# Two-way attention and experts on one core: the output projection of a batch and its residual issued one round later, ahead of the next projections

## The reference

```python
qkv   = layernorm(x) @ Wqkv + bqkv
qkv_a = ctx @ Wqkv_aux + bqkv_aux
q, k, v = split_heads(qkv);  _, ka, va = split_heads(qkv_a)      # 16 heads of 8
p  = softmax(q @ k.T * scale);  pa = softmax(q @ ka.T * scale)
gate = sigmoid(g)                                               # one per head
att = (p @ v) * (1 - gate) + (pa @ va) * gate
x = x + tanh(g_xattn) * (att @ Wo + bo)
# then: x = x + tanh(g_ffn) * experts(layernorm(x)), 64 experts, 8 per token, and one shared expert
```

## Time and profile before

| what | value |
|---|---|
| time, median of 3 runs | 875.36 us (871.0 to 877.55) |
| time of the profiled execution | 874.03 us |
| its span in the trace | 872.2 us |
| granted TensorE clock | 1.0 of full speed throughout |
| PE / DVE / ACT / POOL busy | 832.4 / 690.8 / 565.8 / 637.7 us |
| batch 2, round 0 to batch 31, round 3 | 56.1 to 301.0 us of the span |

### The profile page before, as it was taken

The page is one execution under the profiler, slowest core; times in us unless marked ns, Lnnn a source line. Parts: engine busy times, 40 slices in busy tenths (PEclk is TensorE's granted clock), DMA queues, the critical chain, the costliest instruction groups (busy, mean ns, idle before and its releaser), DMA issues.

```text
span 872.2 us, 20170 instructions
## 1 busy us (share of the span) xinstructions
PE 832.4 (95%) x6733; PEld 646.8 (74%) x6733; DVE 690.8 (79%) x1656; ACT 565.8 (65%) x964; POOL 637.7 (73%) x602
## 2 busy tenths in 40 slices
PE   5899999998898889999999999999999999999997
PEld 3467777776675668888888888887888888888885
DVE  6789899998888858778777877967976977877655
ACT  4377888887777756566566567548557556656554
POOL 2476888887883357887787786887787788778785
PEclk9999999999999999999999999999999999999999
DMA  5567777777653156646554654654746555655552
GB/s 131 175 173 188 182 192 189 186 193 182 168 156 81 32 138 151 151 119 148 134 134 123 168 133 109 169 129 110 179 119 143 145 134 126 148 131 140 143 137 58
DMA packets 113747, 125.27 MB, mean 144 GB/s; under 512 B 28000, under 2 KB 76064, under 8 KB 112208
## 3 DMA queue, kind: packets, MB, share of 16 engines
q1 hardware_dynamic: 110768, 123.47, 56.8%
q10 hardware_dynamic: 2880, 0.59, 0.4%
HBM read 103.55 MB, written 19.96 MB: 142 GB/s over the span
## 4 chain that ended last, share of the span: by engine, by line
PE 75%; DMA 6%; DVE 2%; issue 2%; ACT 2%; POOL 1%; SPq 0%; DVEq 0%; ACTq 0%; POOLq 0%
PE bank L1963 20%; PE bank L1965 20%; PE bank L1964 20%; PE bank L1305 4%; DMA stack_q<-nmaxT 3%; PE bank L1292 3%; PE bank L1279 2%; DMA stack_k<-k_scratch 1%; PE bank L1261 1%; PE bank L1249 1%; DMA cwb<-wts_scratch 1%; ACT prob L787 1%; PE bank L1313 1%; PE bank L1940 1%; PE bank L1326 1%
## 5 line engine op out<-in xcount | busy, mean ns | idle before, releaser
L1640 POOL TENSOR_TENSOR hid<-act,cwb 128x512 f32<-128x512 f32 x264 | 424.4, 1616 | 125.7 <-DVE act L1867 71.7
L1693 ACT ACTIVATE silu<-bank 128x512 f32<-128x512 f32 x256 | 152.8, 597 | 193.7 <-PE bank L1965 189.2
L1867 DVE TENSOR_TENSOR act<-silu,bank 128x512 f32<-128x512 f32 (+1 forms) x264 | 180.5, 684 | 118.8 <-ACT silu L1693 76.6
L1963 PE MATMUL bank<-xhi,weights_hi 128*128 128x512 f32 x520 | 206.7, 397 | 0.4 <-ACT silu L1693 0.4
L1875 DVE TENSOR_TENSOR hlo<-hid,hhi 128x512 fp32r<-128x512 f32 x256 | 199.4, 779 | 7.3 <-ACT hhi L1699 7.0
L1965 PE MATMUL bank<-xlo,weights_hi 128*128 128x512 f32 x520 | 204.1, 392 | 0.0
L1964 PE MATMUL bank<-xhi,weights_lo 128*128 128x512 f32 x520 | 203.8, 392 | 0.0
L984 DVE TENSOR_REDUCE mx<-bank 128x4 f32<-128x512 f32 x256 | 167.5, 686 | 22.4 <-PE bank L1279 18.7
L1699 ACT ACTIVATE hhi<-hid 128x512 fp32r<-128x512 f32 (+1 forms) x264 | 165.0, 625 | 13.3 <-POOL hid L1640 10.9
L787 ACT ACTIVATE prob<-bank 128x1024 f32<-128x1024 f32 x128 | 131.0, 1024 | 64.0 <-PE bank L1292 61.8
L1965 PEld LDWEIGHTS bank<-xlo,weights_hi 128*128 128x128 f32 x520 | 97.6, 188 | 22.0
(11 more groups left out here) (235 smaller groups left out, 1003.0 us busy)
## 6 DMA issues: line engine op xcount, KB each, us to landing
cwb<-wts_scratch SPq DMA_DIRECT2D x174, 384.0 KB, 5.4
stack_k<-k_scratch SPq DMA_DIRECT2D x30, 384.0 KB
k_scratch<-parts_k SPq DMA_DIRECT2D x15, 384.0 KB, 3.3
stack_q<-q_scratch SPq DMA_DIRECT2D x30, 192.0 KB
k_scratch<-parts_k SPq DMA_DIRECT2D x15, 256.0 KB, 3.9
q_scratch<-parts_q SPq DMA_DIRECT2D x15, 192.0 KB, 2.2
xin<-in_x_dram SPq DMA_DIRECT2D x16, 128.0 KB, 2.5
cin<-in_ctx_dram SPq DMA_DIRECT2D x16, 128.0 KB, 2.6
```

The costliest lines, as they stand in the source:

```text
L1640: pool.tensor_tensor(h_buf[k][:], a_buf[k][:], cwb[slot][:, q % GP, :], ALU.mult).then_inc(h_ok, 1)
L1693: act.activation(s_buf[k % RS][:], g_bank[k % 2][:], ACT.Silu).then_inc(s_ok, 1)
L1867: nc.vector.tensor_tensor(a_buf[k % RS][at], s_buf[k % RS][at], u_bank[k % 3][at], ALU.mult).then_inc(a_ok, 1)
L1963: nc.tensor.matmul(bank, w[0], mh, start=first, stop=False)
```

## The change

`out_proj(b - 1)` leaves round 3 of batch b; it is issued in round 0 of batch b + 1, behind `weighted` and in front of `project_qk`, `project_v` and `turn_max`. Its residual on VectorE leaves unit 7 (the end of round 3) and stands in unit 1 of the next batch, between `maxima` and `evac_nmax`. Only in the last batch does the projection of batch 30 stay in round 3. No instruction is added or taken away.

```diff
@@ on_dve
                         minus_max(b + 1, 1 - odd, min(n + 3 + odd, NC))
+                    if u == 1 and b > 1:
+                        residual(b - 2, (b - 2) // CH, (b - 2) // CH % 2, odd)
                     if u == 1 and one_more:
                         evac_nmax(b + 1)
...
-                    if u == 7 and not first:
-                        residual(b - 1, *((n, i, 0) if odd else (n - 1, 1 - i, 1)))
+                    if u == 7 and b == NB - 1:
+                        residual(b - 1, n, i, 0)
@@ on_pe
                             weighted(b - 1, 1 - odd, u + UNITS - LAG, n if odd else n - 1, i if odd else 1 - i)
+                    if r == 0 and b > 1:
+                        out_proj(b - 2, odd)
                     if r == 0 and odd and n + 3 < NC:
                         wait(pe, v_ev, n + 2)
                         project_qk(n + 3, 1 - i)
...
-                    if r == 3 and not first:
+                    if r == 3 and b == NB - 1:
                         out_proj(b - 1, 1 - odd)
```

## The result

The changed kernel takes **890.9 us** (median of 6 runs, 882.29 to 892.71) against 875.17 for the kernel before (6 runs): a ratio of 1.0186 with a 95% interval of 1.0155 to 1.0217, that is 1.9% slower. The forecast was 886, slower.

A forecast was written before the change was run, and what follows sets the result against it. Each round was bound by the longer of ScalarE's path and TensorE's list, not TensorE's total work. Compute +9.9 and shift DMA +0.9 gave +10.8 on 874.03, or 884.8; expected median 886 us, band 881 to 891, overall range 877 to 894.

The forecast's parts named there:

- rival (b): Round 0 and shift DMA: opening paid twice, lead costs in full; about +17 us, median 893 (889 to 898); chance 0.16.
- Round 0, +11.2: TensorE's list binds round 0, so two added matmuls cost 0.43 us in each of 26 batches: 11.2 us.
- The opening: TensorE weight loads idle 0.20 us when a 128-wide step follows 32-wide `weighted`; `out_proj` would pay it instead of round 0's projection.
- Round 3, -1.3: Removing `out_proj` shortens round 3 from 1.85 to ScalarE's 1.76 us: 0.09 gained in 14 even batches, 1.3 us.
- VectorE and SP, 0: The moved residual fills VectorE waiting time; the later `store_x2` and the SP queue behind it cost nothing.
- Late shift DMAs, +2.8: Shift DMA needed at round 0: `stack_k` issued further ahead makes it late more often, 9.0 against 6.2 us.
- 1.1 + s: Lead of `stack_k` over the shift DMA in odd batches, growing from about 0; stall s is 0.7 us.
- Waits for `stack_k`, -1.9: `stack_k` loads issued earlier relative to their need remove TensorE's waits for them, gaining 1.9 us.
- Rival (a): DMA queues: longer batches let them empty in time, stalls shrink; half gone +5.8 us, median 881 (876 to 883); chance 0.29.
- Rival (c): TensorE's sum of work is the bound: 0.21 us saved in each of 30 batches, -6.3, median 869; chance 0.03.
- the one on tiling: Skill page: changing tiling mode drains TensorE; by it the change gains, one such turn per batch going away.
- the one on DMA queues: Skill page: DMA engines alternate queues packet by packet, so shift DMA stalls would not grow; sum near +9.9 us.

The follow-up runs named there:

- The early wait: Changed kernel with TensorE's wait for the odd batches' shift DMA taken in front of `weighted` of round 3: 883.37 us, ratio 1.0169.
- the wait on SP: SP waits for the odd batch's round 1 scores before loading `stack_k`: on the changed kernel 877.37 us, ratio 1.0077; on the kernel before 869.23, 0.9978.
- the filler: Changed kernel with the projection's two matmuls also issued in round 3, without semaphore: 886.21 us, ratio 1.0154; measured again 884.48, 1.0153.

## Why the prediction was right, and where its sum was short

The sign, the mechanism in round 0 and the range held; the size was short, 10.8 us forecast against 18.7 between the two profiled executions (16 by the ratio). The 890.9 lies at the upper edge of the forecast's own band (881 to 891) and inside that of rival (b) (889 to 898), and it got there by a term that neither had.

- **Round 0, +11.2:** right. 0.45 a round instead of 0.43; 26 rounds give 11.6. The opening is paid once.
- **Round 3, -1.3:** wrong, it gives nothing. The step that failed is the gain of 1.85 - 1.76: the first score of a batch has two waits in front of it, and its handover is 0.15, not 0.06. The rows showed the 0.15 already; I took it for TensorE's lateness. The early wait brought the 1.76 back.
- **VectorE and SP, 0:** right, by the kernel that moves the residual alone, and by the one with the projection behind `turn_max`.
- **Late shift DMAs, +2.8:** right in size, 9.3 us against 6.2, or +3.1, and in part by luck; that the lead of `stack_k` does it in most cases is shown by the wait on SP. But the leads did not start from about 0 (in the kernel before they go from -1.06 to 1.78), and they were no even 1.1 + s: in eight odd batches they were 1.0 to 2.8, in one 0.8, and in four the loads went out in the batch before, 4.2 to 5.3 us ahead, which did no harm. Instead of 12 waits, 11 of them of 0.7, there were eight, of 1.2 on the mean and up to 1.9. (The 5.05 us from issue to need is 5.07 by its rows; nothing hangs on it.)
- **Waits for `stack_k`, -1.9:** they did go. The rounds 0 of even batches were nevertheless stretched, by the clock.
- **What was missing, +7.6:** the lower clock in five rounds 0 and part of two rounds 1. I had the parts of the idle time, a hole left in round 3 plus stalls, and costed it as if idle time were all it cost. In the profiles with the filler and with the wait on SP no round runs at the lower clock.

From the start of batch 2 to the start of the last round of attention these terms are 11.6 + 3.1 + 7.6 - 1.9 = 20.4, and the traces show 265.2 - 244.9 = 20.3 us; the program's start up to batch 2 was 1.8 shorter in this execution, which no experiment follows up.

Rival (a), queues that empty in time, is out as a whole, since the stalls grew; in four odd batches its picture holds, the pair was through before the shift DMA came. Rival (b) is out in its mechanism: the opening is paid once, and the late DMAs cost 3.1 more and not 8.6; that its band holds the measured time is due to the clock. Rival (c), TensorE's sum, is out: TensorE's work fell by the openings, and the time rose. Of the two pages of the Trainium skill that the prediction names, the one on tiling fits the opening, but the saving by it does not reach the time here, since round 3 is bound by ScalarE; turns packet by packet, as the one on DMA queues has it, do not explain why the first packet of the small transfer starts only 2.2 to 4.7 us after its issue behind the pair. How often the clock falls differs from run to run. It cost 7.6 us in the first profiled execution (mean clock 0.990) and about 3 in the second (0.996); by the clocks of all 12 executions its mean cost is some 3 to 5 us, an estimate.

## What to carry to other kernels

Work that sits in a slack in front of a wait is free, and moving it to a stage that is already bound by the same engine costs its time there in full, less what the neighbours share (here the opening); ask for each stage which of the two sides of the lockstep is longer, not how busy the engine is. A hole opened in front of a wait that is sometimes long can cost more than the wait: in these traces TensorE's clock then often fell. And when a stage's pace changes, ask which transfer now overtakes which.

## What the runs showed of the hardware

- In the changed kernel's first trace, TensorE idle for 1.79 to 2.55 us before a round was followed five times by a round at a mean granted clock of 0.60 to 0.73, in which the same matmuls took 3.62 to 4.30 us instead of 2.71. In other traces 1.86 and 2.02 us were followed by full clock, and 1.20 and 1.64 by a fall.
- The first score of a batch, with waits on the exponential and on the shift DMA in front of it, started 0.15 us after the exponential; with the second wait taken earlier, 0.06.
- A 16 KB DMA issued 1.0 to 2.2 us behind a pair of 384 KB loads on the other queue started its first packet 2.2 to 4.7 us after its issue in the changed kernel and came too late for a need 5 us later; issued 0.01 us behind their first, its first packet started after 1.3 us and its last ended after 1.5 to 2.0; issued 4.2 to 5.3 us behind them, it ended after 1.9 to 2.7.
